# Turning a pair's sums and the next pair's maxima in one bank, in a fused attention and feed-forward kernel

## The reference

```
xn = layernorm(x) * g1 + b1;  q, k, v = split(xn @ w_in.T + b_in)      # 16 heads of 16
scores = q @ k.T / 4;  row r sees all columns if r % 8 == 0, else only column r
x = x + softmax(scores) @ v @ w_out.T + b_out
x = x + gelu(layernorm(x) @ w1.T + b1) @ w2.T + b2                     # 256 -> 1024 -> 256
x = layernorm(x_in + x)
top = argmax(x @ gate_W.T + gate_b)                                    # one of 8 experts
x = layernorm(x + relu(x @ wi.T + wi_b + lora[top](x)) @ wo.T + wo_b)
```

## Time and profile before

| | |
|---|---|
| median of 3 runs | 1442.03 us (1438.64 to 1444.67) |
| the profiled execution | 1439.25 us, of which the span is 1437.5 us |
| TensorE busy | 1364.4 us, 95% of the span |
| VectorE busy | 852.9 us, 59% |
| ScalarE busy | 732.3 us, 51% |
| GpSimd busy | 647.6 us, 45% |
| chain that ended last | TensorE 78%, VectorE 8%, GpSimd 5% |
| granted clock of TensorE | 0.993 on average |

### The profile page before, as it was taken

The page is one execution under the profiler, slowest core; times in us unless marked ns, Lnnn a source line. Parts: engine busy times, 40 slices in busy tenths (PEclk is TensorE's granted clock), DMA queues, the critical chain, the costliest instruction groups (busy, mean ns, idle before and its releaser), DMA issues.

```text
span 1437.5 us, 26427 instructions
## 1 busy us (share of the span) xinstructions
PE 1364.4 (95%) x10103; PEld 1073.2 (75%) x10103; DVE 852.9 (59%) x1823; ACT 732.3 (51%) x1103; POOL 647.6 (45%) x533
## 2 busy tenths in 40 slices
PE   6799999999999999999999999999999999999997
PEld 5688665578888766668888866667888866557886
DVE  6747566746656576655647566753665656663332
ACT  3444555553444555654444466555344455556442
POOL 3554321337764323246865422334776432132755
PEclk9899999999999999999999999999999999999999
DMA  7565123216662132212672213311566212310100
GB/s 243 162 177 108 39 50 78 56 34 194 192 146 71 35 76 51 57 44 90 204 214 69 66 34 80 71 40 35 192 190 148 72 42 42 77 26 30 52 16 30
DMA packets 91393, 130.49 MB, mean 91 GB/s; under 512 B 8314, under 2 KB 68180, under 8 KB 88148
## 3 DMA queue, kind: packets, MB, share of 16 engines
q1 hardware_dynamic: 91268, 128.82, 32.9%
HBM read 68.08 MB, written 60.57 MB: 90 GB/s over the span
## 4 chain that ended last, share of the span: by engine, by line
PE 78%; DVE 8%; POOL 5%; issue 4%; ACT 2%; DMA 0%; SPq 0%; POOLq 0%; DVEq 0%; ACTq 0%
PE ps L1659 19%; PE ps L1660 16%; PE ps L1661 16%; PE ps L1848 8%; PE ps L1837 7%; PE ps L1822 4%; PE ps L1895 2%; PE ps L1917 2%; PE ps L1883 2%; POOL rows L1122 2%; DVE stats L1404 2%; DVE mx L1530 1%; DVE x1in L1425 1%; DVE xn L1492 1%; ACT prob L1260 1%
## 5 line engine op out<-in xcount | busy, mean ns | idle before, releaser
L1530 DVE TENSOR_REDUCE mx<-ps 128x2 f32<-128x1024 f32 x256 | 311.1, 1223 | 177.4 <-PE ps L1822 174.4
L1260 ACT ACTIVATE prob<-ps 128x1024 f32<-128x1024 f32 x256 | 262.1, 1024 | 156.9 <-PE ps L1837 156.1
L1137 POOL TENSOR_TENSOR hid1l<-gel,hid1h 128x512 fp32r<-128x512 f32 x85 | 111.2, 1308 | 207.3 <-ACT hid1h L1302 207.0
L1137 POOL TENSOR_TENSOR hid0l<-gel,hid0h 128x512 fp32r<-128x512 f32 x86 | 112.2, 1305 | 184.9 <-ACT hid0h L1302 184.8
L1137 POOL TENSOR_TENSOR hid2l<-gel,hid2h 128x512 fp32r<-128x512 f32 x85 | 110.8, 1304 | 168.6 <-ACT hid2h L1302 168.5
L1294 ACT ACTIVATE gel<-ps,cols 128x512 f32<-128x512 f32 x128 | 88.1, 688 | 181.2 <-PE ps L1661 170.0
L1296 ACT ACTIVATE gel<-ps 128x512 f32<-128x512 f32 x128 | 76.5, 598 | 140.4 <-PE ps L1917 139.9
L1837 PEld LDWEIGHTS ps<-qslot,kslot 50*128 50x128 f32 x1024 | 76.4, 185 | 82.2 <-issue 46.0
L1837 PE MATMUL ps<-qslot,kslot 50*128 50x256 f32 x1024 | 129.4, 331 | 4.0 <-ACT prob L1260 3.6
L1848 PE MATMUL ps<-prob,vals 128*32 128x256 f32 x2048 | 124.6, 382 | 0.0
L1822 PE MATMUL ps<-kslot,qslot 48*128 48x512 f32 x512 | 102.7, 411 | 7.9 <-DVE mx L1530 7.5
(11 more groups left out here) (246 smaller groups left out, 3972.2 us busy)
## 6 DMA issues: line engine op xcount, KB each, us to landing
k_d<-kst SPq DMA_DIRECT2D x192, 128.0 KB
kslot<-k_d SPq DMA_DIRECT2D x64, 384.0 KB
xin<-in_L_attn_x SPq DMA_DIRECT2D x32, 256.0 KB, 4.4
rows<-xs_d SPq DMA_DIRECT2D x16, 512.0 KB, 6.1
y_d<-rows SPq DMA_DIRECT2D x15, 512.0 KB, 3.1
rows<-y_d SPq DMA_DIRECT2D x15, 512.0 KB, 4.5
out<-rows SPq DMA_DIRECT2D x15, 512.0 KB, 3.2
xs_d<-xin SPq DMA_DIRECT2D x28, 256.0 KB, 3.1
```

The costliest lines, as they stand in the source:

```text
L1137: nc.gpsimd.tensor_tensor(hid[i % RING][1][:], gel[i % 2][:], hid[i % RING][0][:], ALU.subtract).then_inc(lo_done, 1)
L1260: nc.scalar.activation(prob[prob_of(*a[1:])][:].rearrange("p e i q -> p (e i q)"), ps[:, 0:2, :].rearrange("p a n -> p (a n)"), ACT.Exp).t ...
L1530: nc.vector.tensor_reduce(best[:, :, j % NQ], ps[:, at:at + 2, :], AX.X, ALU.max).then_inc(maxr_done, 1)
```

## The change

Five things are edited.
- `turns`: at kk = 4 of pair p one entry holds `ot` of pair p - 1 (if there is one) and, behind it, `mt` and `mtd` of pair p + 1 (if there is one). Before, `ot` became an entry at kk = 1 and `mt` at kk = 4, at the head.
- `turned_out` has no conditions left. It is called in part 2 of an item without a hook, and in the last part of every item, there after the first down product of half 1 and no longer right after `ev`. The call ahead of `pi` is gone.
- `mt` writes columns 256 to 383 of the bank and `ot` columns 0 to 255. `EARLIER` gives an `mt` that follows an `ot` in its bank no wait. ScalarE's copy of the sums then waits for both turns (`WITH_OT`).
- In batches 0 and 3 the hooks are in the items f = 1, 3, 5, 7 of a block, before in 0, 2, 4, 7.
- The jobs `sum` are put at place 0 (half 0) and 1 (half 1) of the job list, before at its end.

```diff
         def turns(s):
             p, kk = s // KK, s % KK
-            if p and kk == 1:
-                alone.append([("ot", b, p - 1)])
-            if kk == 4 and p + 1 < PAIRS:
-                alone.insert(0, [("mt", b, p + 1), ("mtd", b, p + 1)])
-
-        def turned_out(s, taken):
-
-            if alone and (alone[0][0][0] == "mt" or len(blocks) == 2 or s % KK in (0, 5, 6, 7) or not taken):
-                if alone[0][0][0] == "ot":
-                    flush("os")
+            if kk == 4:
+                alone.append([("ot", b, p - 1)] * (p > 0) + [("mt", b, p + 1), ("mtd", b, p + 1)] * (p + 1 < PAIRS))
+
+        def turned_out():
+
+            if alone:
+                flush("os")
                 for one in alone.pop(0):
                     put(one)
                     if one[0] == "ot":
                         job(1.3, ("os", *one[1:]))
-                return True
-            return taken
...
-                job(0.7, ("sum", blk, h))
+                jobs.insert(h, (0.7, unit[0], (("sum", blk, h),)))
...
-        places = [(0, 2, 4, 7)] * 2 if len(blocks) == 2 else [(0, 2, 3, 7), (0, 1, 3, 7), (1, 2, 4, 7)]
+        places = [(1, 3, 5, 7)] * 2 if len(blocks) == 2 else [(0, 2, 3, 7), (0, 1, 3, 7), (1, 2, 4, 7)]
...
-                taken = bool(hook)
                 if hook and hook[0][0] == "pi":
                     flush("pick")
-                    if alone and alone[0][0][0] == "mt":
-                        turned_out(s, False)
...
                 if not hook:
-                    taken = turned_out(s, False)
+                    turned_out()
             if part == parts - 1:
                 put(("ev", i))
-                turned_out(s, taken)
                 one = pending.pop(0)
                 down_part(one, 1, 0)
+                turned_out()
...
-            if _n in _latest and _latest[_n] not in EARLIER[_s]:
+            if _w == "mt" and _latest[_n][0] == "ot":
+                WITH_OT[_latest[_n][1:]] = _s[1:]
+            elif _n in _latest and _latest[_n] not in EARLIER[_s]:
                 EARLIER[_s].append(_latest[_n])
...
                 elif what == "ot":
                     n = N("ot", *a)
                     act.wait_ge(oturn_done, n)
+                    if a in WITH_OT:
+
+                        act.wait_ge(mturn_done, N("mt", *WITH_OT[a]))
```

More of the change, by code:

```diff
@@ L559, in bank_of @@
     return OUT
-BANK, EARLIER = {}, {}
+BANK, EARLIER, WITH_OT = {}, {}, {}
 _latest = {}
@@ L1232, in step @@
                         act.wait_ge(mcp, 32 * (n - 1))
-                    nc.scalar.activation(mT[:], ps[0:2 * UNITS, BANK[(what, *a)], 0:P], ACT.Copy).then_inc(mt_done, 1)
+                    nc.scalar.activation(mT[:], ps[0:2 * UNITS, BANK[(what, *a)], QW:QW + P], ACT.Copy).then_inc(mt_done, 1)
                 elif what == "ot":
@@ L1826, in step @@
                     pe.wait_ge(negs_done, 2 * N("ng", *a))
-                    nc.tensor.transpose(ps[0:2 * UNITS, bank, 0:P], negs[:].rearrange("p e h t -> p (e h t)"), ident[:]
+                    nc.tensor.transpose(ps[0:2 * UNITS, bank, QW:QW + P], negs[:].rearrange("p e h t -> p (e h t)"), ident[:]
                                         ).then_inc(mturn_done, 1)
```

## The result

The changed kernel takes 1401.47 us (median of 5 runs, 1400.15 to 1401.99), the kernel before 1438.69 us beside it (median of 5, 1438.50 to 1444.67): the ratio of the two means is 0.9727, with a 95% interval of 0.9707 to 0.9747. The forecast was 1410, with a range of 1401 to 1425: the direction and the places were right, and the gain was larger than said, down to the edge of the range. The profiled execution took 1400.15 us, its span is 1398.4 us, 39.1 less than before.

The account below looks back on a forecast made before the run. TensorE, 95% busy, was taken as the bound, so only its standing still pays: 35.5 us gained less 4.0 given back took 1439.25 to 1407.75, about 1410 with 2.8 for the median; range 1401 to 1425.

Parts of the forecast that it names:

- covers that just hold: Batches 0 and 3, up product behind the row turns: cover barely suffices, 8 x 0.25 = 2.0 us charged as lost.
- ScalarE's order: Sums' copy now ahead of the hidden half's, next exponential some 0.4 us later: 1.2 us lost in batches 0 and 3.
- the clock: Short TensorE idles may lower the clock; some 1.7 us more would go, put only into the range's lower end.
- The signs at the prediction's end: If right: listed waits gone, attention stages of batches 0 and 3 about 13 us shorter each, batches 1 and 2 4 to 5.
- Part 1: Batches 0 and 3: maxima's turn no longer waits behind row turns (13.3 us gained) or gate products (2.0); 2.0 lost.
- Part 2: Sums and maxima turned together in one bank: 6.0 us gained, 1.2 more at the pick turn, 0.8 lost there.
- Part 3: Batches 0 and 3: sums' turn precedes the next "or", so VectorE's copy no longer delays maxima steps; 9.3 us gained.
- Part 4: Batches 1 and 2: block sums queued before the statistics, so first down products wait less for their bank; 3.7 us gained.
- The first (waits move to VectorE): Half the two-block batches' gain (24.6 us) returns as maxima-step waits for VectorE's mx: 1422 us; chance 0.16.
- The second: Up product behind the rows' turn waits as mt did; the 13.3 us gain shrinks to a third: 1419 us; chance 0.08.
- the fourth: Next up still finds the bank taken, by two copies, and the gain is returned there: 1440 us; chance 0.03.
- The third: Pair turn waits for late maxima; whole gain gone from 2.5 us lateness, 1460 us at 3.2 us late; chance 0.03.

Follow-up runs that it names:

- no_pair_bank: The changed kernel in its whole order, but mt waits for ScalarE's copy of ot like any other user of the bank; 1416.20 us, ratio 0.9827.
- two_oraw: The kernel before, in its own order, with a second buffer for oraw, so "or" waits for ot of two pairs before in the pairs covered; 1430.72 us, ratio 0.9939.
- sums_last: The changed kernel with the block sums put at the end of the job list as before; 1405.93 us, ratio 0.9748.
- late_maxima: The changed kernel with two more unused VectorE reductions ahead of each pair's last maximum, pairs 1 to 7 of each batch; 1438.22 us, ratio 0.9980.
- load_behind: The changed kernel with two more unused VectorE reductions right behind the negated maxima, pairs 1 to 7; 1446.46 us, ratio 1.0036.
- up_first_sums: The changed kernel with half the first up product ahead of each attention's second score step, and both block-sum halves as one job; 1400.99 us, ratio 0.9713.

## Why the prediction was nearly right, and where it fell short

By the stages: an undisturbed execution of before has 148.7 + 167.0 + 167.0 + 148.4 = 631.1 us of attention, the changed kernel 598.1. That is 33.0, where the sum had 31.5. The waits that it named went where it said, but for two of 0.25 us. Two steps failed, both terms of the sum that were put at a wrong size:

- what is given back for covers that just hold, 2.0 us for the up product behind the row turns and 1.2 us for ScalarE's order, 3.2 in all. The runs show nothing of it;
- the clock, put at nothing in the sum. It was worth 1.4 us in the attention of the profiled pair, 1.9 on the average of the traces, and some 7 us in whole executions (estimate below).

That the stages miss by only 1.5 us is partly luck. For batches 0 and 3 the terms make 6.65 + 1.0 + 0.6 + 4.65 - 1.6 = 11.3 us each, and 12.8 and 12.9 were measured: without the charges of 1.6 they come out right. For batches 1 and 2, which have four of the ten waits of ot each, they make 2.4 + 0.6 - 0.4 + 1.85 = 4.45 each, and 3.7 was measured. So 3.1 us too little and 1.6 too much stand against each other. The signs at the prediction's end (about 13 us and 4 to 5) do not go with its own sum: they make 34 to 36.

- **Part 1, 13.3 and 2.0 less 2.0 back: the gain right, the loss wrong.** The pauses alone are worth 12.7, and four waits for gcopy are gone. Nothing came back: in batches 0 and 3 no up product waits for a row turn. The changed kernel in batch 3, in order of time (answering):

```profile
1159.57 0.60 PE L1880 MATMUL ps<-ident,rows 128*128 128x128 f32 x4
...
1160.83 0.69 DVE L1597 TENSOR_TENSOR turned1l<-ps,turned1h 128x512 fp32r<-128x512 f32 x1 [0.75 <-ACT turned1h L1264]
...
1161.44 1.21 DVE L1527 TENSOR_REDUCE mx<-ps 128x2 f32<-128x1024 f32 x1
...
1161.58 0.49 PE L1656 MATMUL ps<-turned0h,wih 128*128 128x512 f32 x1
```

  The subtraction ends at 1161.52, the up product starts at 1161.58 with no idle time. The reduction is held up until 1161.44 by the subtraction, as I had said, but no maxima step waits for it. Charging each near miss 0.1 to 0.25 us was the step that failed: a cover that just holds costs nothing. The same goes for the 1.2 us for ScalarE's order, since the score product waits 3.5 us before and after.
- **Part 2, 6.0 and 1.2 less 0.8: the mechanism right, the price of a wait too high.** Both turns follow each other at 0.22 us, the copies at 0.18, ahead of the hidden half's (answering):

```profile
1166.75 0.16 DVE L1542 TENSOR_TENSOR negs<-negm,negs 128x4 fp32r<-128x4 f32 x1
...
1168.30 0.38 PE L1851 MATMUL ps<-ident,oraw 128*128 128x128 f32 x2
...
1168.52 0.27 PE L1824 MATMUL ps<-ident,negs 128*8 128x128 f32 x1
...
1168.87 0.28 ACT L1236 ACTIVATE osum<-ps 128x136 f32<-128x136 f32 x1 [0.48 <-PE ps L1824]
1169.05 0.25 ACT L1227 ACTIVATE mT<-ps 8x128 f32<-8x128 f32 x1
...
1169.32 0.63 ACT L1299 ACTIVATE hid0h<-gel 128x512 fp32r<-128x512 f32 x1
```

  The sums' copy is indeed released by the maxima's turn. A wait between the two costs 0.49 us by no_pair_bank and not 0.6, which is 1.1 us less for the ten that went in batches 1 and 2, most of the 1.6 that they lack. In the changed order the shared bank is worth 11.8 us, since the pair meets 24 times there; the sum rightly counts only the 12 waits that before had. The new wait for ust is 1.1 us of idle load in two places, 0.8 said.
- **Part 3, 9.3: right**, by two_oraw (9.1, with one of the eight long waits still there). The copy now waits only for its own sums, 0.67 us in place of the 2.50 of the earlier trace rows:

```profile
1158.21 0.42 DVE L1551 COPY oraw<-ps 128x256 f32<-128x256 f32 x1 [0.67 <-PE ps L1845]
```

- **Part 4, 3.7: about right.** The waits fell by 3.1 us, from 5.2 to 2.1: in each of the two stages the largest and one of 0.25 us are left, where none but the largest was said. In the changed order the early sums are worth 4.8 (sums_last). The wait of the earlier trace rows shrank from 1.46 to 0.81, the statistics being out of the way:

```profile
599.69 0.68 DVE L1609 TENSOR_TENSOR rows<-rows,ps 128x512 f32<-128x512 f32 x1
...
600.42 0.19 PEld L1656 LDWEIGHTS ps<-wfh,hid0h 128*128 128x128 f32 x1 [0.81 <-DVE rows L1609]
```

  What I had not seen: in each of batches 1 and 2 a maxima step now waits 0.38 us (idle load; 0.18 of the matmul), where a run of pick steps delays a reduction.
- **The clock** was the term that I left out of the sum and gave only to the lower end, at 1.7 us. The attention has four stretches of 1.4 us in the three traces of before and none in the two of the changed kernel, 1.9 us on average. In whole executions it is more. The 38 of before beside the experiments have a mean span of 1438.5 us at a mean clock of 0.9901, the five of the changed kernel 1399.4 us at 0.9948: 39.1 us apart. Span times clock, an estimate of the time at full clock, is 1424 and 1392, 32 apart, so some 7 us are the clock. Where these stretches lie is not shown, as no trace of those executions is kept.
- **Rivals.** The first (waits move to VectorE) didn't happen, but late_maxima and load_behind show how near it was: 2.3 us more work per pair takes all of the 33 us back. The second and the fourth are shown wrong by the rows above. The third put the loss of the whole gain at maxima 2.5 us late, by waits of the turn for them; the margin left is 1.39 us here (1168.30 less 1166.91). In late_maxima 2.3 us were enough, but only 9.5 of the 34 us are such waits, the rest are waits of the maxima step and of block sums.

From the 1407.75 of the sum to the 1400.15 of the profiled execution 7.6 us are missing: 1.5 by the stages, 1.4 by the half-clock stretch in batch 3, and 4.7 that lie where the change does nothing (3.2 ahead of the first attention, 1.5 between the stages). These 4.7 are luck; a part of the 3.2 is a half-clock stretch at 85.5 us, which the second trace of the changed kernel has too, at 83.1. The rest up to 1410 is the 2.8 us that I added for the median of three. The median of before came out at 1438.69 in five, and the changed kernel's lies 1.3 us above its profiled execution. Its executions hardly differ (1400.15 to 1401.99 us, clock 0.994 to 0.995), while the 38 of before go from 1433.77 us at 0.994 to 1449.55 at 0.984. So what I added was probably time at the lower clock too; this is argued and not shown.

## What to carry to other kernels

When several small steps share a bank, list who opens it after whom in the written order: two users in one item cost a whole evacuation, and moving one of them by an item cost nothing here. Look also at what a step in another engine's queue waits for: a copy that waits for a later turn of TensorE holds up all that is queued behind it, and TensorE then waits for VectorE although VectorE is idle. Don't charge for covers that are merely thin where the rows show that they hold; test by a stage's length, which repeats to 0.1 us, rather than by whole times. But look at the clock of all executions and not only of the profiled one: here it carries, by the estimate above, some 7 of 39 us, and the stages of an undisturbed trace hide it.

## What the runs showed that I had not expected

Eight pauses of 1.65 us in a TensorE that is 92% busy came with stretches at half clock, 1.4 us lost in each, in all five traces that have them, and with a mean clock of 0.990 to 0.992 over all executions in place of 0.994 to 0.995. So such a pause can cost more than its length. What else has to come together for a stretch is left open. The first exponential of a stage waits for a table load of 1.28 us on ScalarE, four times in before and in the changed kernel as well. It makes the exponential late, and with it the second score step, whose matmul waits 0.88 us for it at each stage's start. The load and the exponential behind it in up_first_sums:

```profile
157.30 1.28 ACT L1263 ACT_TABLE_LOAD   x1
...
158.60 1.02 ACT L1263 ACTIVATE prob<-ps 128x1024 f32<-128x1024 f32 x1
```
